# A transformer decoder layer on one core: the value products of the second attention, step by step through another ring

## The reference

```
x = layernorm(x + first_attention(x))           # 16 heads, bf16, after a convolution
x = layernorm(x + second_attention(x, ctx))     # 16 heads of 16 columns, float32
x = layernorm(x + routed_feed_forward(x))
```

```
y  = softmax(causal(q  @ k.T  * scale)) @ v     # self:  512 queries, 512 keys
y += softmax(       qc @ kc.T * scale ) @ vc    # cross: 512 queries, 1024 context keys
return y @ Wp + bp
```

## Time and profile before

| | before |
|---|---|
| median of 3 runs | 2302.18 us (2301.65 to 2310.58) |
| profiled execution, span from first to last instruction (the page gives no other time of it) | 2303.2 us |
| PE busy | 2183.0 us (95%) |
| DVE busy | 1869.5 us (81%) |
| ACT busy | 1384.6 us (60%) |
| POOL busy | 189.0 us (8%) |
| mean granted TensorE clock | 0.97 of full speed |

### The profile page before, as it was taken

The page is one execution under the profiler, slowest core; times in us unless marked ns, Lnnn a source line. Parts: engine busy times, 40 slices in busy tenths (PEclk is TensorE's granted clock), DMA queues, the critical chain, the costliest instruction groups (busy, mean ns, idle before and its releaser), DMA issues.

```text
span 2303.2 us, 37677 instructions
## 1 busy us (share of the span) xinstructions
PE 2183.0 (95%) x13138; PEld 991.3 (43%) x13138; DVE 1869.5 (81%) x5137; ACT 1384.6 (60%) x2977; POOL 189.0 (8%) x349
## 2 busy tenths in 40 slices
PE   5999999999999999999999999999999999989992
PEld 2354434543345434554335543454334543345432
DVE  6858879788888879788797887978888787978854
ACT  2834687456854579446783467745686457844560
POOL 3011001100011000110001100010001100001000
PEclk7899999999999999999999999999999999999995
DMA  3600034000520006100160002500043000510000
GB/s 110 130 10 1 1 67 81 10 1 1 113 44 10 1 19 121 27 1 1 38 119 10 2 1 58 100 10 1 1 91 57 10 1 11 105 33 1 1 10 9
DMA packets 250845, 81.69 MB, mean 35 GB/s; under 512 B 236064, under 2 KB 247328, under 8 KB 250656
## 3 DMA queue, kind: packets, MB, share of 16 engines
q1 hardware_dynamic: 250656, 79.29, 16.8%
HBM read 16.35 MB, written 4.19 MB: 9 GB/s over the span
## 4 chain that ended last, share of the span: by engine, by line
PE 79%; DVE 10%; ACT 7%; issue 3%; DMA 0%; SPq 0%; POOL 0%; DVEq 0%; POOLq 0%; ACTq 0%
PE bank L1517 23%; PE bank L1570 13%; PE bank L1555 7%; PE bank L1204 7%; PE bank L1513 5%; ACT work L603 4%; PE bank L1552 4%; PE bank L1470 4%; DVE work L770 4%; PE bank L1333 3%; PE bank L1320 2%; PE bank L1356 2%; PE bank L1530 2%; PE bank L1582 1%; ACT k_c L636 1%
## 5 line engine op out<-in xcount | busy, mean ns | idle before, releaser
L659 ACT ACTIVATE work<-bank 128x512 f32<-128x512 f32 (+3 forms) x1536 | 739.7, 550 | 529.8 <-PE bank L1552 264.1
L1033 DVE TENSOR_REDUCE top_half<-bank 128x1 f32<-128x512 f32 x1024 | 625.5, 682 | 21.0 <-PE bank L1517 21.0
L1517 PE MATMUL bank<-k_c,q_c 32*128 32x512 f32 x2048 | 628.6, 634 | 0.0
L1555 PE MATMUL bank<-q_c,k_c 32*128 32x512 f32 x2048 | 526.2, 633 | 0.0
L603 ACT ACTIVATE work<-work,neg 128x512 bf16<-128x512 bf16 x512 | 362.6, 715 | 30.5 <-DVE work L770 29.8
L1517 PEld LDWEIGHTS bank<-k_c,q_c 32*128 32x128 f32 x2048 | 274.6, 184 | 245.1 <-DVE top_half L1033 159.8
L770 DVE TENSOR_SCALAR_CACHE_REDUCE work<-bank 128x512 bf16<-128x512 f32 x512 | 322.4, 686 | 43.7 <-PE bank L1302 33.6
L1570 PE MATMUL bank<-work,v_flat 128*32 128x512 f32 (+3 forms) x3072 | 321.8, 544 | 5.5 <-ACT work L659 5.0
L1030 DVE CUSTOM_DVE_ANT_0 masked<-bank,mask_w 128x384 bf16<-128x384 f32 (+3 forms) x512 | 223.8, 488 | 79.5 <-PE bank L1513 74.0
L1552 PE MATMUL bank<-q_s,k_s 32*128 32x512 f32 (+3 forms) x1024 | 258.1, 471 | 0.0
L1555 PEld LDWEIGHTS bank<-q_c,k_c 32*128 32x128 f32 x2048 | 218.4, 183 | 78.4 <-ACT work L659 48.6
(11 more groups left out here) (194 smaller groups left out, 2214.1 us busy)
## 6 DMA issues: line engine op xcount, KB each, us to landing
xT_pad<-xT SPq DMA_DIRECT2D x16, 256.0 KB, 3.3
ctx_sb<-ctxT SPq DMA_DIRECT2D x8, 512.0 KB, 3.4
x_res<-x SPq DMA_DIRECT2D x8, 512.0 KB, 4.8
out<-r_sb SPq DMA_DIRECT2D x8, 512.0 KB, 3.1
work<-work SPq DMA_TRANSPOSE x112, 4.4
qk_sb<-qkT SPq DMA_DIRECT2D x1, 512.0 KB, 4.7
pe_sb<-pe_w SPq DMA_DIRECT2D x1, 256.0 KB, 4.0
v_sb<-vT SPq DMA_DIRECT2D x1, 256.0 KB, 5.4
```

What stands on the lines that cost most here:

```text
L659: nc.scalar.activation(pT[:, s % PT_SLOTS, g, q0:S], exp_bank(n)[:, 0:S - q0], ACT.Exp, scale=SCALE).then_inc(pT_ready, 1)
L1033: nc.vector.tensor_reduce(top_half[:, i % 2, g, u // 2, u % 2:u % 2 + 1], scores, AX.X, ALU.max, negate=True).then_inc(slot_out, 1)
L1517: mm(dst, q_c[rows, i, P * t:P * (t + 1)], k_c[rows, i, S * half:S * (half + 1)], start=True, stop=True, tile_position=(GW * g, 0)).then_i ...
L1555: mm(dst, k_c[rows, i, P * u:P * (u + 1)], q_c[rows, i, :], start=True, stop=True, tile_position=(GW * g, 0)).then_inc(sT_mm, 1)
```

## The change

In steps 0 to 35 each step's value products go by themselves. `parts_behind(s)` names the part that falls due at the end of step s: that of step s-2 in the self steps and of step s-1 in the cross steps. `pv_part(p)` multiplies the step's four heads into a slot of ACT's ring (banks 4 to 7), which now has five uses a step, four transposed scores and one part. `part_out(p)` lets ACT copy the slot to SBUF: straight into `o_rows` if the part is the first of its head group, else into one of two halves of `featB`. `add_part(p)` lets POOL add that half to `o_rows`. DVE's copies and adds of bursts 0 to 8 go; from burst 9 on its reads stay, the first of them with a wait for all of POOL's adds. `o_rows` now alternates between two halves of `featA` by head group.

More of the change, by code:

```diff
@@ L96, in decoder_layer @@
     FFN_USES = 1
-    USES = ALL_SCORES + (4 + BURSTS) * HG + FFN_USES
     EXPERT_LEAD, GATHER_LEAD, SPLINE_LEAD = 1, 2, 3
@@ L327, in outputs_behind, with adds_before, part_columns, last_part @@
             return [(kind, i) for kind in (SELF, CROSS) for i in range(HG) if BURST * (bursts_of(kind, i)[-1] + 1) + 3 == s]
-        def burst_behind(s):
-            return [s // BURST - 1] if s % BURST == 0 and s > 0 else []
+        def parts_behind(s):
[3 more added lines that the diff above has]
+            return part_of(PART * p)[2] == 0
+        def adds_before(p):
+            return sum(not opens_rows(a) for a in range(p))
+        ADDS = adds_before(PARTS)
+        def part_columns(p):
+            kind, _, u = part_of(PART * p)
+            return slice(P * u if kind == SELF else 0, S)
+        def o_rows(kind, i):
[3 more added lines that the diff above has]
+            return (o_rows(kind, i) if opens_rows(p) else featB[:, adds_before(p) % 2, :])[:, part_columns(p)]
+        def last_part(kind, i):
+            return (first_step(kind, i) + (NT if kind == SELF else NC)) // PART - 1
         def outputs_ready(s):
@@ L375, in decoder_layer, with exp_ring_bank, part_bank @@
         LAST_BURST = ALL_STEPS // BURST - 1
+        def exp_slot_uses():
[4 more added lines that the diff above has]
+            return order
+        exp_order = exp_slot_uses()
+        exp_uses = {name: n for n, name in enumerate(exp_order)}
+        assert len(exp_order) == FIRST_LATE + PARTS
+        def exp_ring_bank(use):
+            return RING + use % EXP_RING
         def exp_bank(n):
-            return bank[:, RING + n % EXP_RING if n < FIRST_LATE else LATE_EXP_BANKS[(n - FIRST_LATE) % len(LATE_EXP_BANKS)], :]
+            return bank[:, exp_ring_bank(exp_uses["exp", n]) if n < FIRST_LATE else LATE_EXP_BANKS[(n - FIRST_LATE) % len(LATE_EXP_BANKS)], :]
+        def part_bank(p):
+            return bank[:, exp_ring_bank(exp_uses["part", p]), :]
         def last_exp(at):
@@ L1043, in outputs @@
                     dve.wait_ge(slot_in, base + use + 1)
-                    if j < HG or j % 2 == 0:
-                        nc.vector.tensor_copy(o_rows[:, SELF if j < HG else CROSS, :], slot(uses, use)).then_inc(slot_out, 1)
-                    else:
-                        dve.wait_ge(slot_out, base + uses["pv", j - 1] + 1)
-                        nc.vector.tensor_tensor(o_rows[:, CROSS, :], slot(uses, use), o_rows[:, CROSS, :], ALU.add).then_inc(slot_out, 1)
+                    rows = o_rows(CROSS, (j - HG) // 2)
+                    if j % 2 == 0:
+                        nc.vector.tensor_copy(rows, slot(uses, use)).then_inc(slot_out, 1)
+                    else:
+                        if j == SINGLES_FROM:
+                            dve.wait_ge(part_added, (b + 1) * ADDS)
+                        else:
+                            dve.wait_ge(slot_out, base + uses["pv", j - 1] + 1)
+                        nc.vector.tensor_tensor(rows, slot(uses, use), rows, ALU.add).then_inc(slot_out, 1)
                 def put_rows(kind, i):
```

36 lines of the change are left out of this document (23 added, 13 removed).

## The result

The changed kernel took 2283.67 us (median of five runs, 2273.5 to 2294.99) against 2307.3 for the kernel before beside it: a ratio of 0.9898, 95% interval 0.988 to 0.9917. It is faster by about 1%, some 24 us. The forecast was 100 us. The profiled execution, the fastest of the five, is shorter by 31.4 us.

The account below looks back on a forecast made before the run. Neither PE nor DVE alone bound the kernel: bursts starved DVE, then PE waited for it. Gains of 5.5 (cross) and 7.0 (self) us over 8 batches make 100 us, from 2303.2 to 2202 us; range 2168 to 2285.

Parts of the forecast that it names:

- Cross steps: Four-step cross cycle falls from 13.76 to 12.65 us, set by PE; five cycles gain 5.5 us a batch.
- Self steps: Four-step self cycle falls from 15.45 to 13.7 us, set by DVE; four cycles gain 7.0 us a batch.
- DVE's tolerance: DVE's ring of four maxima, 2.4 us, lets it tolerate a late PE; a score's way takes about 1.15.
- Four cycles of 15.45: One self cycle measured at 15.45 us was counted four times a batch, each gaining 1.75 us.
- Late steps "at nothing": Late steps keep their instructions and were costed at nothing in either direction.
- GpSimd's adds: Adds of parts into the output rows, 1.3 us each, under a step of 2.95 us, costed at nothing.
- rival 4: GpSimd's adds hold DVE up, 1.2 us for each of 17 cross-step adds: 2389 us, chance 0.03.
- rival 3: Fourth transposed score falls out of its set, PE doing it alone: 101 us slower, 2403 us, chance 0.06.
- 27 adds a batch: GpSimd's count of adds per batch, one per step at most, beside 16 causal selections.
- rival 1: ACT's copy or signal 0.25 us later a turn, self steps half: 56 us more, 2258 us, chance 0.17.
- Rival 5: No change, 2302 us, as DVE's waits return elsewhere; sign: early stage shorter, late steps longer by as much; chance 0.04.

Follow-up runs that it names:

- e12: Changed kernel with the convolution two steps later and, in the self steps, both groups of transposes one step on: 2279.38 us (0.9872).
- e9: Changed kernel with the self steps' value products computing only the 128 columns of the diagonal tile; one run, 2226.67 us.
- e10: As e9, with only one transpose of four for the self outputs as well; one run, 2234.71 us.
- e14: Changed kernel with the convolution two steps later and only the self outputs' transposes moved one step on: 2268.31 us (0.9825).
- e13: Changed kernel with the convolution two steps later and the self steps' parts one step behind instead of two: 2260.90 us (0.9789).
- e2: Products by single steps only in self steps 0 to 15, cross steps' bursts as in the kernel before: 2313.77 us (1.0025 of the kernel before).
- e3: Changed kernel with DVE's convolution for the batch after next two steps later, behind the read of burst 9: 2272.85 us (0.9834).
- e11: Changed kernel with the convolution two steps later and, in self steps 0 to 7, each step's last transposed score computed twice: 2283.73 us (0.9895).
- e8: Changed kernel with parts of two steps instead of one, each product twice as long: 2304.36 us (0.9993 of the kernel before).
- e6: Changed kernel with only the first of four heads computed in the self steps' value products; one run, 2279.63 us.

## Why the prediction was wrong

**Cross steps: right in the mechanism, near in the size.** Four steps take 12.84 or 13.06 us, forecast 12.65. Steps 20 to 37 gave 6.3 us a batch, forecast 5.5 for the cross cycles; the forecast counted from copy to copy, so that burst 8 at the end of step 36, where half of the gain lies, is in it.

**Self steps: the step that failed.** The text put DVE's tolerance at "four maxima of 0.60 us = 2.4 us, of which a score's way to DVE takes about 1.15", which leaves 1.25 us for a product of 1.0, and it let DVE set the cycle with 0.1 us a step for hand-overs. The rows of e12 put it otherwise: when PE issues its last score before a product, DVE has 2.04 us in hand (1.81 at another break), and ahead of the product lie another 0.52 us. That leaves 2.04 - 1.16 - 0.52 = 0.36 us, which only a product of 128 columns keeps to (0.36 from its start to PE's next score in e9). Longer absences add to DVE's time, 1.06 us of idle time a cycle, where the forecast took the larger of PE's sum (12.5) and DVE's. DVE's own figure was nearly right: forecast 13.7 with hand-overs, 13.82 in e9 and e10, where the absences are short.

Theory H, that PE is simply full, foretold the cycles of e9, e12 and e14 as well or better. Against it stand e13, where a cycle with the same work of PE took 14.72 us and not 14.95 (though steps 0 to 20 as a whole were no shorter), and PE's waits for DVE's slots within the cycle. That the length of the products costs the time is shown (e9). How it does is read from the timelines, whose sums give the idle time to 0.02 us at the four breaks worked out above; no run changes PE's sum and leaves its absences as they are.

**Four cycles of 15.45: mis-sized too.** The cycle shown stood for all four. The first four steps had no burst in them and took 10.21 us; with parts they take 12.23. The others gained 0.27, 0.49 and 0.70 us, and e2 shows the last burst's share coming off steps 16 to 20. In e9, where DVE's pace is reached, steps 0 to 20 take 51.96 + 12.50 = 64.46, 3.8 us less than the 68.27 before; the forecast had 8.1 (7.0 and one cross cycle). So the sum could not have been reached with DVE as the bound either.

**Late steps "at nothing": wrong.** The instructions are the same, but the list on DVE takes 12.3 us before and after, and set against step 37 it now starts 1 us later. PE's wait for the read of burst 9 grew from 1.00 to 1.85 us, and in four of five such batches the lower clock followed. e3 shows it: 11 us back by the medians from moving one item of the list, and 217.2 to 201.5 us of late steps by the traces.

**The rivals.** GpSimd's adds of 512 columns took 1267 ns (forecast 1.3 us) and the maxima 681 ns as before, so rival 4 did not come; nor did rival 3. The prediction's 27 adds a batch are 29 (12 in the self steps, 17 in the cross steps; 232 ran), which changes nothing in its sum. ACT's copies waited for products 50.2 us in all, over 101 of 288. The time is that of rival 1 at 1.5 times its price (2285), but not by its mechanism: what was late was PE for DVE, not ACT's copy for PE, for which PE's weight loads waited once in the whole run, 0.2 us. Rival 5's sign, "the early stage shorter but the late steps longer", was right for nearly a quarter of the early gain (11.9 of 51.8).

The groups of instructions (count, busy us, mean ns, idle before):

```profile
L591 POOL TENSOR_TENSOR featA<-featA,featB 128x512 f32<-128x512 f32 x136 | 172.3, 1267 | 330.1 <-ACT featB L735 330.1
L1110 DVE TENSOR_REDUCE top_half<-bank 128x1 f32<-128x512 f32 x1024 | 631.4, 681 | 69.1 <-PE bank L1600 68.1
```

**Open.** What makes the clock fall in the self steps. Falls came in some batches and not in others under equal busy time, came with more work for PE too (e11), and with shorter products in none of eight batches (e9) and one of eight (e10); with products twice as long there were two (e8). These are counts of one trace each. On the changed kernel they cost about 10 us of its gain in the profiled run.

## What to carry to other kernels

Two engines that feed each other through a short ring did not take the larger of their two sums here: count for each break what the consumer has in hand at the producer's last item, and take from it the gap ahead of the break, the break, and the way of the next item. A break cost nothing where the consumer had work of its own as long beside it (PE's transposes of 0.59 us, DVE's read of 0.69). And when a stage gets shorter, look at the engine that runs a fixed list through its end: a wait that was short there can grow.

## What the hardware showed that was not expected

The four heads' value products, in four column strips of PE, take as long as one: 0.85 and 0.83 us for 384 columns (e6); columns count, heads do not. After a wait of 1.85 us PE ran the next product at half speed, 1.86 us for 1.00, and after one of 2.06 us in another batch at full speed. And the clock fell to 0.54 in one batch and stayed at 1.00 in the next with the engines equally busy for the 24 us before.
